# Delivering the last expert tile's rows by matmul, in a two-layer attention and mixture-of-experts kernel

## What is computed

```python
logits = xf @ router_w.T                      # xf: 1024 tokens x 256, 8 experts
top_vals, top_idx = jax.lax.top_k(logits, 2)
top_w = jax.nn.softmax(top_vals, axis=-1)
combine = jnp.sum(jax.nn.one_hot(top_idx, 8) * top_w[..., None], axis=1)
for e in range(8):
    h = jax.nn.silu(xf @ Wg[e].T) * (xf @ Wu[e].T)      # 688 hidden
    out = out + combine[:, e:e + 1] * (h @ Wd[e].T)
```

## Time and profile before

| what | us |
|---|---|
| median of 3 runs (lowest, highest) | 914.49 (914.37, 918.74) |
| the profiled execution, device time | 916.71 |
| its span, first to last recorded instruction | 914.5 |
| PE busy | 792.4 (87% of the span) |
| DVE busy | 363.3 (40%) |
| ACT busy | 289.8 (32%) |
| POOL busy | 224.9 (25%) |
| queue 1 (SP): 54.56 MB | 20.9% of 16 engines' span |
| queue 0 (POOL): 30.97 MB | 9.2% of 16 engines' span |

### The profile page before, as it was taken

How to read it: one execution, slowest core, us unless ns; L and a number is a source line. 1 busy time by engine, 2 the same in 40 slices (tenths; PEclk the granted TensorE clock), 3 DMA queues, 4 the chain that set the end, 5 groups by cost and what they waited for, 6 DMA issues and landing times.

```text
span 914.5 us, 14815 instructions
## 1 busy us (share of the span) xinstructions
PE 792.4 (87%) x5020; PEld 603.2 (66%) x5021; DVE 363.3 (40%) x902; ACT 289.8 (32%) x527; POOL 224.9 (25%) x260
## 2 busy tenths in 40 slices
PE   1989799999989999999945389989887999999990
PEld 0767587777767677777733257767664767777770
DVE  8444154543533312222136486676542422212211
ACT  1102103114233333433213214445453244334311
POOL 8341013333131411212123400011312422112123
PEclk9999899999999999999986779999997999999995
DMA  7953914223962216110220731211301110011004
GB/s 233 394 130 98 319 64 93 59 49 89 371 201 67 70 55 207 40 34 24 63 93 17 196 80 34 57 44 35 142 29 53 58 36 34 23 34 34 29 18 143
DMA packets 48123, 88.09 MB, mean 96 GB/s; under 512 B 8913, under 2 KB 37329, under 8 KB 45937
## 3 DMA queue, kind: packets, MB, share of 16 engines
q1 hardware_dynamic: 36743, 54.56, 20.9%
q0 software_dynamic: 7568, 30.97, 9.2%
q10 hardware_dynamic: 3760, 1.87, 0.7%
HBM read 52.04 MB, written 35.03 MB: 95 GB/s over the span
## 4 chain that ended last, share of the span: by engine, by line
PE 80%; DVE 8%; DMA 5%; issue 2%; ACT 2%; POOL 1%; SPq 1%; ACTq 0%; POOLq 0%; DVEq 0%
PE bank L1389 24%; PE bank L1416 13%; PE bank L884 9%; PE bank L463 4%; PE bank L508 4%; PE bank L1402 4%; PE bank L519 2%; PE bank L453 2%; PE bank L537 2%; PE bank L506 2%; PE bank L580 2%; DVE stat L328 2%; PE bank L554 1%; DMA q_parts<-XN 1%; DVE XN L600 1%
## 5 line engine op out<-in xcount | busy, mean ns | idle before, releaser
L1389 PE MATMUL bank<-wgu,R 128*128 x736 | 226.2, 460 | 0.5 <-ACT R L1424 0.4
L1389 PEld LDWEIGHTS bank<-wgu,R 128*128 128x128 f32 x736 | 138.1, 193 | 66.2 <-issue 4.2
L1416 PE MATMUL bank<-R 112*128 (+1 forms) x552 | 127.0, 379 | 1.2 <-ACT R L1438 1.2
L1454 DVE TENSOR_TENSOR R<-R,bank 128x344 f32<-128x344 f32 x92 | 47.2, 513 | 181.9 <-PE bank L1389 171.2
L1416 PEld LDWEIGHTS bank<-R 112*128 112x128 f32 (+1 forms) x552 | 104.4, 190 | 22.3 <-issue 1.7
L651 ACT ACTIVATE PTR<-bank 128x512 f32<-128x512 f32 x144 | 83.5, 597 | 97.7 <-PE bank L508 82.6
L1365 POOL DMA_INDIRECT rows_out<-R,XN x46 | 45.9, 999 | 170.7 <-ACT R L1446 159.0
L1461 DVE COPY R<-bank 112x512 f32<-112x512 f32 x46 | 31.7, 690 | 103.7 <-PE bank L1402 103.7
L600 DVE TENSOR_REDUCE XN<-bank 128x2 f32<-128x512 f32 x96 | 63.1, 684 | 10.7 <-PE bank L463 10.7
L1432 ACT ACTIVATE R<-bank 128x344 f32<-128x344 f32 x92 | 41.9, 457 | 76.8 <-PE bank L1389 76.6
L1446 ACT ACTIVATE R<-bank 128x256 f32<-128x256 f32 x46 | 17.7, 385 | 146.7 <-PE bank L1416 146.7
(11 more groups left out here) (170 smaller groups left out, 1280.1 us busy)
## 6 DMA issues: line engine op xcount, KB each, us to landing
wgu<-in_wgu SPq DMA_DIRECT2D x10, 1376.0 KB, 11.5
slots_in<-PTR POOLq DMA_DIRECT2D x1, 9088.0 KB, 26.0
row_of_slot<-in_unused POOLq DMA_DIRECT2D x2, 4544.0 KB, 17.4
R<-slots_in SPq DMA_DIRECT2D x46, 128.0 KB, 2.0
wgu<-R SPq DMA_DIRECT2D x32, 128.0 KB, 2.4
R<-R SPq DMA_DIRECT2D x32, 128.0 KB, 2.4
R<-in_wd SPq DMA_DIRECT2D x8, 448.0 KB
PTR<-rows_out SPq DMA_DIRECT2D x12, 256.0 KB, 4.1
```

What stands on the lines that cost most here:

```text
L1389: last = nc.tensor.matmul(BK[2 * half + gu][:, 0:IH], xsT[:, p, kk, :], wgu[:, bass.ds(e * (KD * GU) + (kk * GU + gu * I + half * IH), IH) ...
L1416: last = nc.tensor.matmul(down_bank(i)[:, 0:D], hT[0:CH[c], p, c, :], wd[0:CH[c], bass.ds(e * (6 * D) + c * D, D)], start=c == 0, stop=c == 5)
L1454: v.tensor_tensor(hh[:, half * IH:(half + 1) * IH], sg[:, half * IH:(half + 1) * IH], BK[2 * half + 1][:, 0:IH], ALU.mult).then_inc(s["hid ...
```

## The change

The last expert tile (tile 22) is no longer scattered to `rows_out`. Instead:

- For each token tile t, VectorE builds a 128x128 matrix with the weight of the token's choice where its slot lies in tile 22, and zero elsewhere (`last_tile_vector`, `sends_vector`). It does this after its work for tiles 19, 20 and 21. TensorE transposes the matrices in two groups of four, one ahead of `tile_up(22)` and one behind it, and ScalarE copies them to SBUF. After `tile_down(22)` TensorE multiplies the tile's results by the eight matrices into four PSUM banks (`deliver_tensor`).
- The first slot of tile 22 is spread to all partitions by a one-column matmul. A small table `iota` is loaded by SP ahead of the loads of tiles 2 and on.
- `wearly` holds the weights with those of pairs in tile 22 set to zero; `combine_scalar` and `combine_vector` use it. `combine_vector` ends, for each sequence, with a wait for GpSimd's adds and for the bank, and one addition of 128x512 from PSUM ("whole"). The statistics and the output DMAs wait for "whole".
- `fetch_sync` waits for the scatters of tiles 0 to 21. Since rows of `rows_out` that belong to tile 22 are now read unwritten, POOL first fills the 2048 rows with zeros: a DMA from `slots_in`, ahead of `number_unused(1)`.
- The four loads of x share two semaphores, so that sequences 1 to 3 wait for all of x. The fetch buffers of token tiles 6 and 7 move.

```diff
@@ -46,6 +46,7 @@
 REST_T = SLOTS_T - FULL_T
+LAST = SLOTS_T - 1
@@ -86,6 +87,7 @@
             "onesb": bf16(np.ones((P, P))), "small": small,
+            "iota": np.broadcast_to(np.arange(P, dtype=np.float32), (P, P)),
@@ -227,8 +229,17 @@
         zeros = PTR[:, 0:FILL]
-        yg = [(PTR[:, 512 * t:512 * t + 512] if t < 6 else XN[:, 512 * t - 2048:512 * t - 1536]).rearrange("p (k d) -> p k d", k=2)
+        yg = [(PTR[:, 512 * t:512 * t + 512] if t < 6 else R2[:, 512 * t + 1504:512 * t + 2016]).rearrange("p (k d) -> p k d", k=2)
               for t in range(NT)]
+        iota = R2[:, 4448:4576]
+        wearly = R2[:, 5600:5616].rearrange("p (k t) -> p k t", k=2)
+        rowl = XN[0:1, 1664:1665].bitcast(BF16)[:, 0:1]
+        first_row = XN[:, 512:513]
+        place = XN[:, 528:544]
+        inside = XN[:, 544:576].rearrange("p (n m) -> p n m", n=2)
+        owned = XN[:, 768:1024].rearrange("p (k s) -> p k s", k=2)
+        sends = vaug[:, :].rearrange("p (t s) -> p t s", t=NT)
+        sendsT = xnT[:, 0, :].rearrange("p (t s) -> p t s", t=NT)
@@ -259,7 +270,7 @@
         s_const = sem("s_const")
-        s_x = [sem(f"s_x{b}") for b in range(B)]
+        s_x = [sem("s_x0"), sem("s_x123")]
@@ -297,7 +308,7 @@
               "slot eid dlt exp1 scatter0 scatter1 xs0 xs1 x_t x_e gu silu hid hid_t hte_v hte_s "
-              "down y_e row0 row1 rows ys0 ys1 g0 g1 g2 g3 weights weighed first added")
+              "down y_e row0 row1 rows ys0 ys1 g0 g1 g2 g3 weights weighed first added whole")
@@ -1193,6 +1204,8 @@
                                         op0=ALU.mult, op1=ALU.add))
+            if not first:
+                link(v.tensor_copy(rowl, rowf[:, n - 1:n]))
@@ -1212,6 +1225,57 @@
             v.tensor_tensor(w01[:, 1, :], ex1, w01[:, 0, :], ALU.mult).then_inc(s["weights"], 1)
+        def last_tile_vector(l):
+            v = nc.vector
+            flat = w01[:, :, :].rearrange("p k t -> p (k t)")
+            early = wearly.rearrange("p k t -> p (k t)")
+            v.wait_ge(FF[l]["consts"], 16 * 6)
+            link(v.tensor_copy(place, slot))
+            link(v.tensor_scalar(place, place, first_row, None, ALU.subtract))
+            link(v.tensor_scalar(inside[:, 0, :], place, 0.0, None, ALU.is_ge))
+            link(v.scalar_tensor_tensor(out=inside[:, 1, :], in0=place, scalar=float(P), in1=inside[:, 0, :],
+                                        op0=ALU.is_lt, op1=ALU.mult))
+            link(v.tensor_tensor(inside[:, 0, :], inside[:, 1, :], flat, ALU.mult))
+            link(v.tensor_tensor(early, flat, inside[:, 0, :], ALU.subtract))
+        def sends_vector(l, tiles):
+            v = nc.vector
+            for t in tiles:
+                link(*[v.tensor_scalar(owned[:, k, :], iota, place[:, k * NT + t:k * NT + t + 1], w01[:, k, t:t + 1],
+                                       ALU.is_equal, ALU.mult) for k in range(TOPK)])
+                both = v.tensor_tensor(sends[:, t, :], owned[:, 0, :], owned[:, 1, :], ALU.add)
+                both.then_inc(FF[l]["weights"], 1)
+                v.wait_ge(FF[l]["weights"], 2 + t)
+        def sends_tensor(l, half):
+            s = FF[l]
+            nc.tensor.wait_ge(s["weights"], 1 + 4 * (half + 1))
+            nc.tensor.wait_ge(s["x_e"], SLOTS_T + half)
+            for t in range(4):
+                last = nc.tensor.transpose(BK[6][:, t * P:(t + 1) * P], sends[:, 4 * half + t, :], ident[:, :])
+            last.then_inc(s["x_t"], 1)
+        def sends_scalar(l, half):
+            s = FF[l]
+            nc.scalar.wait_ge(s["x_t"], SLOTS_T + 1 + half)
+            nc.scalar.activation(sendsT[:, 4 * half:4 * half + 4, :], BK[6][:, :].rearrange("p (t s) -> p t s", t=4),
+                                 ACT.Copy).then_inc(s["x_e"], 1)
+        def deliver_tensor(l):
+            s = FF[l]
+            nc.tensor.wait_ge(s["hid"], 2 * SLOTS_T)
+            nc.tensor.wait_ge(s["x_e"], SLOTS_T + 2)
+            nc.tensor.wait_ge(s["y_e"], SLOTS_T)
+            for t in range(NT):
+                last = nc.tensor.matmul(BK[t // 2][:, (t % 2) * D:(t % 2 + 1) * D], sendsT[:, t, :], yo[:, LAST % 2, :],
+                                        start=True, stop=True)
+                if t % 2:
+                    last.then_inc(s["down"], 1)
@@ -1261,6 +1325,7 @@
             nc.tensor.wait_ge(FF[l]["eid"], 2)
+            nc.tensor.matmul(BK[7][:, 0:1], onesb[0:1, :], rowl, start=True, stop=True).then_inc(FF[l]["rank"], 1)
@@ -1287,6 +1352,8 @@
             weights_vector(l)
+            nc.vector.wait_ge(FF[l]["rank"], B + 1)
+            nc.vector.tensor_copy(first_row, BK[7][:, 0:1])
@@ -1324,7 +1391,7 @@
             if b == 0 and l == 1:
-                nc.gpsimd.wait_ge(s_slots, 16)
+                nc.gpsimd.wait_ge(s_slots, 16 * 2)
@@ -1481,9 +1548,16 @@
             step(SLOTS_T - 2, (SLOTS_T - 2) // 2, 1)
-            step(SLOTS_T - 1, (SLOTS_T - 1) // 2, 0, nxt=False)
-            tile_hidden(l, SLOTS_T - 1, (SLOTS_T - 1) // 2, 0)
-            tile_down(l, SLOTS_T - 1, (SLOTS_T - 1) // 2, 0, expert_of(SLOTS_T - 1))
+            n, p = LAST // 2, LAST % 2
+            e, before = expert_of(LAST), expert_of(LAST - 1)
+            tile_hidden(l, LAST - 1, n + p - 1, 1 - p)
+            sends_tensor(l, 0)
+            tile_up(l, LAST, n, p, e)
+            sends_tensor(l, 1)
+            tile_down(l, LAST - 1, n + p - 1, 1 - p, before)
+            tile_hidden(l, LAST, n, p)
+            tile_down(l, LAST, n, p, e)
+            deliver_tensor(l)
@@ -1497,14 +1571,26 @@
             step(SLOTS_T - 2, (SLOTS_T - 2) // 2, 1)
-            step(SLOTS_T - 1, (SLOTS_T - 1) // 2, 0, nxt=False)
-            tile_scalar_2(l, SLOTS_T - 1, (SLOTS_T - 1) // 2, 0)
-            tile_scalar_y(l, SLOTS_T - 1, (SLOTS_T - 1) // 2, 0)
+            n, p = LAST // 2, LAST % 2
+            tile_scalar_2(l, LAST - 1, n + p - 1, 1 - p)
+            sends_scalar(l, 0)
+            tile_scalar(l, LAST, n, p)
+            tile_scalar_y(l, LAST - 1, n + p - 1, 1 - p)
+            sends_scalar(l, 1)
+            tile_scalar_2(l, LAST, n, p)
+            tile_scalar_y(l, LAST, n, p)
...
         def experts_vector(l):
-            with nc.vector.Fori(2, (SLOTS_T - 1) // 2) as r:
+            with nc.vector.Fori(2, (SLOTS_T - 5) // 2) as r:
...
                 tile_vector(l, 2 * r + 2, r + 1, 0)
+            for i in range(SLOTS_T - 4, SLOTS_T):
+                tile_vector(l, i, i // 2, i % 2)
+                if i == LAST - 3:
+                    last_tile_vector(l)
+                elif i < LAST:
+                    half = i - (LAST - 2)
+                    sends_vector(l, range(4 * half, 4 * half + 4))
@@ -1520,6 +1606,7 @@
                     load_down(e)
+            nc.sync.dma_start(iota, dr["iota"]).then_inc(s["consts"], 16)
@@ -1544,22 +1631,22 @@
             nc.gpsimd.wait_ge(s["rows"], 16 * (TOPK * NT + 1))
-            for i in range(3, SLOTS_T):
-                tile_gpsimd(l, i, i // 2, i % 2, nxt=i + 2 < SLOTS_T)
+            for i in range(3, LAST):
+                tile_gpsimd(l, i, i // 2, i % 2, nxt=i + 2 < LAST)
...
             s = FF[l]
-            nc.sync.wait_ge(s["ys0"], 16 * ((SLOTS_T + 1) // 2))
-            nc.sync.wait_ge(s["ys1"], 16 * (SLOTS_T // 2))
+            nc.sync.wait_ge(s["ys0"], 16 * ((LAST + 1) // 2))
+            nc.sync.wait_ge(s["ys1"], 16 * (LAST // 2))
...
         def output_sync(t):
-            nc.sync.wait_ge(FF[3]["added"], t + 1)
+            nc.sync.wait_ge(FF[3]["whole"], t // 2 + 1)
@@ -1567,20 +1654,24 @@
             if b == 0:
-                nc.scalar.wait_ge(s["weights"], 1)
+                nc.scalar.wait_ge(s["weights"], 2)
...
                 nc.scalar.activation(yg[t][:, 1, :], yg[t][:, 1, :], ACT.Copy,
-                                     scale=w01[:, 1, t:t + 1]).then_inc(s["weighed"], 1)
+                                     scale=wearly[:, 1, t:t + 1]).then_inc(s["weighed"], 1)
...
                 v.wait_ge(s[f"g{t // 2}"], 16 * 2)
-                v.scalar_tensor_tensor(out=xres[:, t, :], in0=yg[t][:, 0, :], scalar=w01[:, 0, t:t + 1],
+                v.scalar_tensor_tensor(out=xres[:, t, :], in0=yg[t][:, 0, :], scalar=wearly[:, 0, t:t + 1],
                                        in1=xres[:, t, :], op0=ALU.mult, op1=ALU.add).then_inc(s["first"], 1)
-            return s["added"], 2 * b + 2
+            v.wait_ge(s["added"], 2 * b + 2)
+            v.wait_ge(s["down"], SLOTS_T + b + 1)
+            xb = xres[:, 2 * b:2 * b + 2, :]
+            v.tensor_tensor(xb, xb, BK[b][:, :].rearrange("p (q d) -> p q d", q=2), ALU.add).then_inc(s["whole"], 1)
+            return s["whole"], b + 1
@@ -1614,7 +1705,7 @@
             for t in range(0, NT, 2):
-                sp.dma_start(xres[:, t:t + 2, :], xd[:, t:t + 2, :]).then_inc(s_x[t // 2], 16)
+                sp.dma_start(xres[:, t:t + 2, :], xd[:, t:t + 2, :]).then_inc(s_x[min(t // 2, 1)], 16)
@@ -1685,6 +1776,9 @@
                 if b == 1:
```

(6 more changed lines are left out.)

## The result

| | median us (lowest, highest) | span of the profiled execution |
|---|---|---|
| before, 7 runs | 914.49 (913.74, 919.97) | 914.5 |
| after, 7 runs | 924.99 (921.26, 928.14) | 922.1 |

The ratio to the kernel before is 1.0085 with a 95% interval of 1.0058 to 1.0111: slower by 5 to 10 us, 7.8 in the middle. Executions of one kernel lie up to 7 us apart, so I read where the time went from distances within a trace, and the total from the ratio.

The account below looks back on a forecast made before the run. The prediction took TensorE's own matmuls, 80% of the span, to bound the kernel. It added 6.7 (fill), 3.3 (layer 1) and 0.2 (end), +10.2 us on 914.49, for 924.7, with a range of 917.5 to 929.

Parts of the forecast that it names:

- The fill's delay: Before sequence 1's first scores: the fill in POOL's queue pushes back L939's transfers, +6.7 us (5.4 to 7.3).
- The Trainium skill's rule of whole packets: At L939's transfers: draining about 9 to 17 descriptors per turn would make the fill cost next to nothing; the trace disagreed.
- Rival (b): At L939's transfers: the fill does not hold them, as more than 1 KB goes through a turn; 918.0 us, chance 0.11.
- The Trainium skill's fit: For the fill: 2.0 us plus bytes over 436 GB/s, an estimate adding 4.8 us and giving 922.3.
- The clock: After the wait before sequence 1's scores: TensorE restarts from the same low clock level, cost 0, at most +1 us.
- Transposes and matrices: Ends of both expert layers: two transpose groups add 0.88 us to TensorE's path; VectorE's matrices, 0.8 us each, stay hidden.
- The fetch 3.5 us earlier: End of layer 3: waiting for tile 21's rows starts the fetch at 892.12 against 895.62.
- the 2.39 us that tile 22 shows from scatter to fetch: Ends of expert layers: tile 22's time from scatter to fetch, 2.39 us, taken for tile 21 too.
- VectorE's turn: In `combine_vector`: waiting for GpSimd's adds makes each sequence take 2.9 us, where the fetch brings one every 2.25 us.
- the cost in layer 1: End of layer 1: VectorE's wait for GpSimd delays `normed_vector(2)` from 491.15 to 494.4, +3.3 us (0 to +4.5).
- The end: End of the kernel: the earlier fetch's gain is given back by VectorE's four turns, +0.2 us (-1 to +1).
- The loads of x: Sequence 1's norm waiting for all of x: its statistics are held to 11.5 by something else, cost 0.

Follow-up runs that it names:

- fill_double: The changed kernel with a second 2 MB fill right behind the first, to rows that later scatters overwrite; 929.46 us in one execution.
- fill_1k: The changed kernel with the fill's pattern rewritten for packets of 1 KB, nothing else; 925.82 us beside 916.17 for before, ratio 1.0091.
- fill_late: The changed kernel with the fill moved behind sequence 0's scatters, as two DMAs copying x instead of zeros; 919.78 us beside 916.17 for before, ratio 1.0031.
- bank_first: The changed kernel with VectorE's addition from PSUM put ahead of GpSimd's adds, which wait for it; 920.86 us beside 916.17 for before, ratio 1.0042.

## Why the prediction was right

The forecast was 924.7, the median is 924.99. That they lie so near is partly luck: by the ratio the loss is 7.8 us (5.3 to 10.2) where I had 10.2, and the kernel before itself measured 916.17, 917.44 and 918.38 later. The direction and both mechanisms held; the terms compare as follows.

- **The fill's delay: +6.7 forecast, 5.7 to 6.3 measured** (10.34, 10.71 and 10.91 less 4.66; fill_double 6.3 more). It lies between the value taken and the lower bound. Mis-sized was the rate: of the two rows I took the slower, 0.29 MB a microsecond, while 2.10 MB in about 6 us is 0.35, near the fill of the slots. The packets slipping through were 32 and not 128, which is too little to matter.
- **The Trainium skill's rule of whole packets** ("DMA: Bandwidth & Descriptors", "Queues, rings and completion order"). Rival (b) hung on a turn of 8 KB or more for SP's queue. The trace has 16 packets of 0.02 MB before and 162 packets of 0.15 MB in fill_1k, 1 KB each: one record of SP's transfers per turn. The Trainium skill's fit ("DMA: Bandwidth & Descriptors", "Anatomy of one DMA"), an estimate, adds 4.8 us for the fill, below the 6 us of the runs. The time by it is 914.5 + 4.8 + 3.5 = 922.8 and not 922.3, inside the interval of the ratio either way.
- **The clock: 0 forecast, 0 measured in this kernel.** TensorE resumed at 114.70 and the slice 119 to 120 shows the rise, 5 us later, as before (107.57, rise by 113):

```profile
114.00:119.00 5.00, 4.30 (x16) 3.64 (x17) 0.74 (x2) 0.00 (x0) 0.00 (x0) 0.50 1.03 402
119.00:120.00 1.00, 1.00 (x5) 0.65 (x4) 0.64 (x1) 0.00 (x0) 0.00 (x0) 0.82 1.09 446
120.00:123.00 3.00, 3.00 (x32) 2.30 (x32) 1.81 (x3) 0.00 (x0) 0.00 (x0) 1.00 1.01 415
```

  The bound of +1 us does not hold for every kernel, though: in fill_1k the 9.7 us at that level cost about 2 us more (an estimate: four matmuls of L463 take 1.71 us at that level and 0.87 at the full one in the kernel before, so half of some 4 to 5 us more is lost).

- **Transposes and matrices: 0.88 forecast.** From tile 21's transposes to the end of the last `tile_down` it is 12.7 us before and 13.5 after, 0.8; ScalarE's 0.1 did not show. A matrix took VectorE 0.96 us (888.21 to 892.04 for four), not 0.8, and stayed hidden: the first product for tile 22 starts at 892.08, the transposes that need the second only at 895.97.
- **The fetch 3.5 us earlier: it was 2.1 (16.29 to 14.19) and 1.9 us (16.31 to 14.38).** The failed step is "the 2.39 us that tile 22 shows from scatter to fetch". In the changed kernel tile 21's scatter took 3.8 and 4.0 us. The DMA queues and issues, 897 to 899, kernel after:

```profile
q0 software_dynamic: 14, 0.06, 6.8%
q8 instruction: 1, 0.02, 3.9%
...
rows_out<-R,XN POOLq DMA_INDIRECT x1, 3.8
```

In both layers a 16 KB instruction packet falls on one of the DMA engines while the scatter runs, and the scatter's last packet of data starts at 3.0 to 3.2 us from issue instead of 1.9. In layer 3 of fill_late the scatter has none in its time, lands in 2.4 us, and the fetch starts 3.5 us earlier (12.79), as forecast. The last scatters of the two layers in all twelve traces go the same way: the ten with no such packet land in 2.40 to 2.46 us, the eleven in which it starts within 1.5 us of the issue in 3.7 to 4.2, and of the three in which it starts at 2.0 two take 4.1 and 4.2 and one 2.4. That the packet is the cause rests on this; no run took it away alone. The trace of before had the number: in layer 1 tile 21's own scatter, issued at 466.08, landed in 4.0 us, and the prediction took tile 22's.
- **VectorE's turn: 2.9 forecast, 2.77 measured,** and the cost in layer 1 +3.3 forecast, +3.6 measured. bank_first took 3.3 of it back. The step in which ScalarE's multiply for sequence 3 stands behind `evac_scalar(0)` is the 2.98 us of idle VectorE before 496.36. Since the fetch started 1.6 us later than I had it and the cost still fits, the two errors partly cancel: the turns were 0.13 us shorter each, and sequence 1's data came 3.12 us after sequence 0's, not 3.5.
- **The end: +0.2 forecast (-1 to +1), -0.1 measured to the end of the span** (35.2 to 35.1), +1.3 to the end of the last output issue, which is what I had forecast. The fetch was 1.4 us later than forecast. That cost nothing because the four turns were 0.13 us shorter each, and because the prediction counted up to the last output issue, while the span ends with GpSimd's last addition: 28.2 us after tile 21's transposes before, 28.3 after. So the number of this term is right partly by luck.
- **The sum.** The spans differ by 7.6 us. Cut at the same instructions, before and after: start to the first `tile_up` of layer 1 272.7 and 278.7, to tile 21's transposes 183.9 and 184.1, to the norm of sequence 2 34.65 and 38.28, to the first `tile_up` of layer 3 203.7 and 202.7, to tile 21's transposes 184.4 and 183.2, to the end of the span 35.2 and 35.1: +6.0, +0.2, +3.6, -1.0, -1.2, -0.1. The three stretches that the change does not lengthen by its own steps (+0.2, -1.0, -1.2) give 2.0 us back together; over the kernels above the second varies from 183.2 to 186.4, the fourth from 201.6 to 204.7 and the fifth from 183.2 to 184.6, so I take their part for the spread of executions. In the first stretch TensorE also reached the old wait 1.4 us later than before (104.35 for 102.91): its first matmuls of L895 took 5.35 us in this execution, 3.91 before (L884) and 3.82 in fill_1k.
- **The loads of x: 0 forecast.** Sequence 1's statistics waited until 6.69 instead of 4.98 and ended at 11.5 in both.
- **Slips in the working that change nothing.** The part of L939's transfers left when POOL's queue is empty is some 900 packets, which at 475 in 2 us is 3.8 us and not "some 5"; four matrices at 0.8 us are 3.2 and not 3.3.

## What to carry to other kernels

A copy that nobody waits for is not free: ask what else is issued within its time, and to which queue, since here one large packet passed for every small one of the other queue. A wait of 4.66 us called "issue" was a DMA, found by adding issue and landing. An addition put behind another engine's result can cost not only its own 0.69 us but everything queued behind the wait; if two additions can change places, the one that waits for nobody goes first. Take the cost of a step from the row of the step itself: the scatter that mattered was tile 21's, 4.0 us in the trace of before, not tile 22's. And measure an end up to what ends the kernel: 1.5 us gained at the last output issue were 0.3 at the end of the span.

## What the runs showed of the hardware that I had not expected

- Three copies from DRAM to DRAM, all written with 128 in front, moved in packets of three sizes: 2 MB as 128 runs of 16 KB, contiguous throughout, in 32 packets of 64 KB; the same as 1 KB rows in 512 packets of 4 KB; `number_unused`, 128 runs of 36 KB, contiguous too, in 128 packets of 36 KB.
- One 16 KB instruction packet beside a scatter of 128 rows goes with 1.3 to 1.8 us more to landing, 3.7 to 4.2 against 2.4 us.
- VectorE's pair of products of 128x256 takes 0.87 us alone and 1.34 to 1.44 us beside GpSimd's adds (bank_first).
- The span ends 6.87 us after GpSimd's last addition in the changed kernel and the seven built from it, whether SP's output DMAs follow that addition at once or later.
